# Ninety unread TensorE products in the long waits of a token-table, attention and feed-forward kernel

## The chip, the cores and the metric

One core of a Trainium2 chip runs one program. The metric is the device time in microseconds from start to end of an execution; shown are three runs and one profiled execution.

## What is computed

`x` holds 8 batches of 512 token ids below 2048. Every id is looked up in a codebook of 2048 rows of 256, sent through a two-layer network, then through one attention layer (16 heads of 64, 4 key/value heads, causal, slopes per head) and one low-rank feed-forward layer, each on a normalised input and with a residual:

```python
h = gelu(codebook[x] @ W1 + b1) @ W2 + b2
n = layernorm(h)
q, k, v = n[..., 128:] @ Wq, n[..., 128:] @ Wk, n[..., :128] @ Wv   # q rotated by an angle per head
att = where(causal, q @ k.T / 8 + slope * rel, -inf)
e = exp(att - max(att)); att = e / (1 + sum(e))
h = h + (att @ v) @ Wo
n = layernorm(h)
h = h + gelu((n @ U1) @ V1 + b1f) @ U2 @ V2 + b2f
```

## The kernel before

The first network depends on the id alone, so it is computed once for each of the 2048 codebook rows. The kernel has two program blocks, one behind the other; all engines leave the first before any starts the second.

**Table stage** (`token_table`). Codebook rows go through in 4 chunks of 512. Per chunk TensorE transposes the rows, makes 8 tiles of the hidden layer (`first_product`, lines 480 to 482) and, two steps behind, adds each into the output rows (`second_product`, lines 495 to 497). Matmul operands are split into a high and a low fp32r part, and three products stand for one. VectorE normalises the finished rows, and they are stored to tables in DRAM, of which `early_rows` and `early_values` serve batch 0 alone. Behind its last product TensorE has nothing to do, while VectorE adds the bias, takes the statistics, normalises, and SyncE stores the last chunk and waits for that store.

**Layer stage** (`layer`). The last chunk's value part is made first: four transposes into bank 2 (line 1164), a split by ScalarE (line 834) and VectorE (line 967) and twelve products (line 1171); ScalarE copies them to `vals`, and SyncE stores them (lines 709 and 711). GpSimd meanwhile issues the gathers of batch 0's rows (line 749, four), then, once the value store has landed, those of its values (four) and those of batch 1 (line 732, four). Then come the `opening` products x, k, q: x transposes the gathered rows (line 1034), k and q are products of three parts each (line 1026), and between x and k, and between q and the first scores, ScalarE copies the high part and VectorE makes the low part.

The main loop runs over slots: 8 batches x 16 heads = 128, and 16 more (`SLOTS` = 144) in which the last batch's projection and feed-forward part are done. In a slot TensorE computes the scores (lines 1130 and 1131), VectorE adds the mask and takes the least value (line 910), ScalarE takes exponentials (line 780), VectorE inverts the sums (lines 917, 919), GpSimd scales (line 744), and TensorE, two slots later, transposes the result (line 1142) and, for two slots at a time, multiplies with the values (line 1158). The feed-forward work of a batch is spread by hand over the slots of the next one, by `first(s)` and `second(s)`: w (output projection), y (transposes of the normalised rows, line 1034), u (first low-rank product, six products, line 1026), f (lines 1104 and 1105) and g (line 1110), d. Each engine works its own queue in order, and semaphores tie them.

For the last batch there are no scores beside it. The projection is done in slots 128 to 131; then VectorE takes statistics (line 876), GpSimd the root, VectorE the normalised rows (line 899), and TensorE goes on with y, u, f and g, d, each behind a copy by ScalarE and a split by VectorE. `ALL` is 128 and `LAG` is 2, so slot ALL + 1 + LAG is 131, and ALL + 8 + LAG is 138.

PSUM has 8 banks of 512 columns. Banks 0 and 1 carry hidden tiles in the table stage and scores in the layer stage; banks 2 to 4 hold the transposed probabilities.

Of the kernel before, what the change touches and what calls it, by code (L numbers as in the profile page):

```python
# [11 lines left out]
P = 128  # L12
ROWS, DIM, HID = 2048, 256, 1024
B, T = 8, 512
# [78 lines left out]
def token_table(nc, part, env):  # L93
# [87 lines left out]
    with nc.Block() as block:  # L181
# [276 lines left out]
        def _(pe):  # L458
# [50 lines left out]
            def make_values(i):  # L509
                pe.wait_ge(tok_low, i + 1)  # L510
                pe.wait_ge(wv_low, 1)
                for t in range(NT):
                    dst = ct_bank(1 - t // 2)[:, t % 2 * DIM:(t % 2 + 1) * DIM]
                    at = slice(t * P, (t + 1) * P)
                    pe.matmul(dst, tok_hi[:, at], wv_hi, start=True, stop=False)
                    pe.matmul(dst, tok_lo[:, at], wv_hi, start=False, stop=False)
                    mm = pe.matmul(dst, tok_hi[:, at], wv_lo, start=False, stop=True)
                    if t % 2 == 1:
                        mm.then_inc(v_full, 1)
# [3 lines left out]
            for n in range(STEPS + BEHIND):  # L523
# [8 lines left out]
                if KH <= n < STEPS and n % KH == VALUES_AT:  # L532
                    make_values(n // KH - 1)

ALL = B * HEADS
SLOTS = ALL + HEADS
O_RING = 10
FF_RING = 4
LAG = 2
# [4 lines left out]
def queries_and_keys(s):  # L544

    out = []
    if s % 2 == 0 and s // 2 + 1 < ALL // 2:
        out.append(("q", s // 2 + 1, 0))
    if s % 4 == 1 and (s + 3) // 4 < ALL // REP:
        out.append(("k", (s + 3) // 4, 0))  # L550
# [14 lines left out]
def second(s):  # L565
# [3 lines left out]
    if i >= 1:  # L569
        b = i - 1  # L570
        if b < B - 1 and 1 + LAG <= j < 1 + LAG + NT:
            out.append(("w", b, j - 1 - LAG))
        if s == ALL + 1 + LAG:
            out += [("w", b, 0), ("w", b, 1)]
# [19 lines left out]
def two_banks():  # L594
# [3 lines left out]
    for s in range(SLOTS):  # L598
        out += [("s", s, j) for j in range(len(UNITS))] * (s < ALL)
        out += [use for use in second(s) if use[0] == "f" and use[2] % 4 < 2]  # L600
        out += [("W", B - 1, m) for m in range(2)] * (s == ALL - 1)
    return out
# [6 lines left out]
def layer(nc, part, env):  # L609

    g = env
    ident, causal, slope, bank, idx = g["ident"], g["causal"], g["slope"], g["bank"], g["idx"]
# [32 lines left out]
    start, rows_in, stored = sem("start"), sem("rows_in"), sem("stored")  # L645
# [59 lines left out]
    with nc.Block() as block:  # L705
# [300 lines left out]
        def _(pe):  # L1006
# [43 lines left out]
            def last_ahead(t):  # L1050

                if t % 2 == 0:
                    ring_opened(("W", B - 1, t // 2))
                pe.wait_ge(o_low, PAIRS * B - 2)
                last_products(t, range(PAIRS - 2))

            def product(kind, n, m):
                if kind == "f" and m % 4 < 2:
                    ring_opened((kind, n, m))
                elif kind == "f" and m == 3:  # L1060
                    pe.wait_ge(o_low, min(PAIRS * (n + 1) + 5, PAIRS * B))
                elif kind == "f" and m == 7:
                    pe.wait_ge(ff_made, KF * n + 4)
                elif (kind != "g" or m == 0) and (kind != "w" or n < B - 1):
                    opened((kind, n, m))
                if kind == "q":
                    cols = slice(2 * n % HEADS * D, (2 * n % HEADS + 2) * D)
                    b = n // PAIRS
                    pe.wait_ge(x_low, b + 1)
                    three(a_of("q", n, 0), [((g["wq_hi"][:, cols], g["wq_lo"][:, cols]), (pos_hi[:, b % 2, :], pos_lo[:, b % 2, :]))])\  # L1070
                        .then_inc(q_full, 1)
                if kind == "k":
                    b, c = divmod(n, KVH)
                    pe.wait_ge(x_low, b + 1)
                    three(a_bank, [((both(g["wk_hi"], c), both(g["wk_lo"], c)), (pos_hi[:, b % 2, :], pos_lo[:, b % 2, :]))])\
                        .then_inc(k_full, 1)
                if kind == "x":
                    if n == 0:
                        pe.wait_ge(first_rows_in, 16 * NT)
                    else:  # L1080
                        pe.wait_ge(rows_in, 16 * NT * n)
                    turn_rows(a_of("x", n, m), pos[:, n % 3, :, :]).then_inc(x_full, 1)
                if kind == "w" and n == B - 1:
                    pe.wait_ge(o_low, PAIRS * (n + 1))
                    last_products(2 * m, range(PAIRS - 2, PAIRS))
                    last_products(2 * m + 1, range(PAIRS - 2, PAIRS)).then_inc(w_full, 2)
                elif kind == "w":
                    pe.wait_ge(o_low, PAIRS * (n + 1))
                    tok = slice(m * P, (m + 1) * P)
                    three(c_bank[:, 0:DIM],  # L1090
                          [((o_hi[:, (PAIRS * n + e) % O_RING, tok], o_lo[:, (PAIRS * n + e) % O_RING, tok]),
                            (g["wo_hi"][:, e, :], g["wo_lo"][:, e, :])) for e in range(PAIRS)]).then_inc(w_full, 1)
                if kind == "y":
                    pe.wait_ge(xn_done, norm_no["y", n])
                    turn_rows(y_bank[m], xn[:, :, m * P:(m + 1) * P]).then_inc(y_full, 1)
                if kind == "u":
                    pe.wait_ge(y_low, KD * (n + 1))
                    three(c_bank, [((both(g["u1_hi"], k), both(g["u1_lo"], k)), (y_hi[:, k, :], y_lo[:, k, :]))
                                   for k in range(KD)]).then_inc(u_full, 1)
                if kind == "f":  # L1100
                    pe.wait_ge(u_low, n + 1)
                    cols = slice(m * P, (m + 1) * P)
                    dst = f_bank(n, m)
                    pe.matmul(dst, g["v1_hi"][:, cols], rank_both[:, :], start=True, stop=False)  # L1104
                    pe.matmul(dst, g["v1_lo"][:, cols], rank_both[:, :], start=False, stop=True).then_inc(ff_full, 1)
                if kind == "g":
                    e = KF * n + m
                    pe.wait_ge(ff_made, e + 1)
                    half = slice(m % 2 * D, (m % 2 + 1) * D)
                    pe.matmul(c_bank[half, :], g["u2"][:, m, :], ff[:, e % FF_RING, :], start=m < 2, stop=m >= KF - 2,  # L1110
                              skip_group_check=True, tile_position=(0, m % 2 * D)).then_inc(ff_used, 1)
                if kind == "d":
                    pe.wait_ge(z_low, n + 1)
                    for t in (2 * m, 2 * m + 1):
                        tok = slice(t * P, (t + 1) * P)
                        mm = three(d_bank[m][:, (t % 2) * DIM:(t % 2 + 1) * DIM],
                                   [((z_hi[:, tok], z_lo[:, tok]), (g["v2_hi"][:, :], g["v2_lo"][:, :]))])
                    mm.then_inc(d_full, 1)
# [44 lines left out]
            for t in range(NT):  # L1163
                mm = pe.transpose(bank(2)[:, t * P:(t + 1) * P], tokens[t], ident[:, :])
            mm.then_inc(tok_full, 1)
            pe.wait_ge(tok_low, 1)
            for t in range(NT):
                at, dst = slice(t * P, (t + 1) * P), value_bank(t // 2)[:, t % 2 * DIM:(t % 2 + 1) * DIM]
                three_v = ((tok_hi, wv_hi), (tok_lo, wv_hi), (tok_hi, wv_lo))
                for n, (tok, wv) in enumerate(three_v):  # L1170
                    mm = pe.matmul(dst, tok[:, at], wv, start=n == 0, stop=n == 2)
                if t % 2 == 1:
                    mm.then_inc(last_full, 1)
            for use in opening:
                product(*use)
            for s in range(SLOTS):
                if s < ALL:
                    scores(s, 0)
                    scores(s, 1)
                for use in first(s):  # L1180
                    product(*use)
                if s == ALL:
                    last_ahead(0)
                if 2 + LAG <= s < ALL + 1 + LAG and (s - LAG) % 2 == 0:
                    values(s - 2 - LAG)
                if s < ALL:
                    scores(s, 2)
                turn_ahead = burst(s) or ("u", s // HEADS - 1, 0) in second(s)
                if turn_ahead and LAG <= s < ALL + LAG:
                    turn(s - LAG)  # L1190
                for use in second(s):
                    product(*use)
                if not turn_ahead and LAG <= s < ALL + LAG:
                    turn(s - LAG)
                if ALL <= s < ALL + NT - 1:
                    last_ahead(s - ALL + 1)


# [24 lines left out]
```

## Time and profile before

| | us |
|---|---|
| median of 3 runs | 969.41 |
| lowest, highest | 963.27, 970.1 |
| profiled execution, whole | 972.13 |
| profiled execution, span from first to last instruction | 970.3 |
| TensorE matmul busy | 869.9 (90%) |
| ScalarE busy | 723.7 (75%) |
| GpSimd busy | 630.2 (65%) |
| VectorE busy | 620.2 (64%) |
| mean granted TensorE clock | 0.970 |

The span is the time from the first to the last instruction in the profile. The granted clock is a share of TensorE's full 2.4 GHz; 0.50 is 1.2 GHz. Matmuls overlap, so that the duration of one is longer than the distance to the next one's start. "Idle before" an instruction is the time that its engine stood still, and the arrow names what ended it.

### The profile page before, as it was taken

Reading aid. Unit: us, or ns where it says so; the run is one execution under the profiler, and the core shown is the slowest. Engines: PE = TensorE matmul, PEld = TensorE weight load, DVE = VectorE, ACT = ScalarE, POOL = GpSimd, SP = SyncE. Lnnn points to the kernel's source line nnn. Section 1 sums busy time; section 2 is a strip of 40 time slices with the busy share of each in tenths; the row PEclk is TensorE's granted clock in tenths of the full one; section 3 lists DMA queues with packets and bytes.
Section 4 is the critical chain, followed back from the end, with each engine's and each line's share of the span. In section 5 each row is a group of like instructions: output and inputs, shape, how many; then the busy total and the mean of one; then the engine's idle time right before and its main releaser. Section 6 shows DMA issues by size and latency. Waiting matters only on the chain.

```text
span 970.3 us, 16896 instructions
## 1 busy us (share of the span) xinstructions
PE 869.9 (90%) x5552; PEld 676.4 (70%) x5552; DVE 620.2 (64%) x1898; ACT 723.7 (75%) x1611; POOL 630.2 (65%) x600
## 2 busy tenths in 40 slices
PE   6999658999989998999899998999899989998976
PEld 5888646777866686578657875787667766786663
DVE  4566636876685768575947584867566775668421
ACT  5754347998788867986889687968787788877813
POOL 6000068899685868587858876787759785768520
PEclk9999959999999999999999999999999999999997
DMA  9333350001000200020001000010001000000000
GB/s 258 67 109 109 115 189 2 1 2 55 2 1 2 76 1 1 1 78 1 1 1 57 22 1 1 23 56 1 1 23 55 2 1 23 1 2 1 1 22 22
DMA packets 23605, 33.55 MB, mean 35 GB/s; under 512 B 2608, under 2 KB 20176, under 8 KB 23520
## 3 DMA queue, kind: packets, MB, share of 16 engines
q1 hardware_dynamic: 19760, 19.01, 6.2%
q0 software_dynamic: 3760, 13.48, 4.9%
q8 instruction: 45, 0.74, 0.3%
q14 instruction: 40, 0.33, 0.1%
HBM read 17.80 MB, written 14.68 MB: 33 GB/s over the span
## 4 chain that ended last, share of the span: by engine, by line
PE 48%; DVE 15%; ACT 12%; issue 7%; POOL 5%; DMA 0%; DVEq 0%; POOLq 0%; ACTq 0%
PE ps L1026 14%; PE ps L1158 11%; PE ps L1142 6%; ACT probs L780 6%; DVE probs L910 5%; PE ps L1130 5%; PE ps L1110 4%; PE ps L1131 4%; POOL probs L744 3%; ACT turned_sb L787 3%; DVE sums L917 2%; DVE o_lo L962 2%; DVE xn L899 1%; PE ps L1104 1%; DVE q_both L927 1%
## 5 line engine op out<-in xcount | busy, mean ns | idle before, releaser
L744 POOL TENSOR_SCALAR probs<-probs,sums 128x512 f32<-128x512 f32 (+3 forms) x512 | 545.7, 1083 | 173.7 <-DVE sums L919 173.3
L910 DVE CUSTOM_DVE_ANT_0 probs<-ps,causal,slope 128x512 f32<-128x512 f32 (+3 forms) x512 | 260.0, 548 | 135.7 <-PE ps L1131 131.8
L780 ACT ACTIVATE probs<-probs,least 128x512 f32<-128x512 f32 (+3 forms) x512 | 282.1, 553 | 25.9 <-DVE least L910 19.0
L1130 PE MATMUL ps<-k_hi,q_both 128*128 128x512 f32 (+3 forms) x512 | 184.2, 360 | 28.1 <-DVE least L910 26.1
L787 ACT ACTIVATE turned_sb<-ps 128x1280 f32<-128x1280 f32 x128 | 157.2, 1228 | 69.6 <-PE ps L1142 69.5
L1158 PE MATMUL ps<-turned_sb,token_rows 128*64 128x512 f32 (+3 forms) x1024 | 152.0, 438 | 19.5 <-ACT turned_sb L787 19.4
L1142 PE MATMUL ps<-ident,probs 128*128 128x128 f32 x1280 | 163.0, 275 | 0.3
L1131 PE MATMUL ps<-k_lo,q_both 128*128 128x512 f32 (+3 forms) x512 | 153.5, 325 | 0.0
L1158 PEld LDWEIGHTS ps<-turned_sb,token_rows 128*64 128x64 f32 x1024 | 75.0, 136 | 104.6 <-issue 87.6
L1130 PEld LDWEIGHTS ps<-k_hi,q_both 128*128 128x128 f32 x512 | 97.8, 191 | 71.7 <-DVE least L910 45.7
L1142 PEld LDWEIGHTS ps<-ident,probs 128*128 128x128 f32 x1280 | 144.2, 141 | 1.5 <-POOL probs L744 1.3
L1131 PEld LDWEIGHTS ps<-k_lo,q_both 128*128 128x128 f32 x512 | 98.2, 192 | 5.0
L780 ACT ACTIVATION_READ_ACCUMULATOR probs<-probs,least 128x1 f32 x512 | 96.3, 188 | 0.0
L927 DVE TENSOR_TENSOR q_both<-ps,q_both 64x512 fp32r<-64x512 f32 x128 | 88.1, 688 | 9.7 <-ACT q_both L797 6.3
L797 ACT ACTIVATE q_both<-ps 64x512 fp32r<-64x512 f32 x128 | 75.4, 589 | 16.0 <-PE ps L1026 14.1
L259 POOL TENSOR_TENSOR row_guess<-row_var,row_power 128x4 f32<-128x4 f32 x4 | 4.1, 1026 | 94.6 <-DVE row_var L360 94.6
L1026 PE MATMUL ps<-wo_lo,o_hi 128*128 128x256 f32 x224 | 62.7, 280 | 0.0
L1026 PE MATMUL ps<-wo_hi,o_hi 128*128 128x256 f32 x224 | 62.7, 280 | 0.0
L1026 PE MATMUL ps<-wo_hi,o_lo 128*128 128x256 f32 x224 | 62.7, 280 | 0.0
L962 DVE TENSOR_TENSOR o_lo<-ps,o_hi 128x512 fp32r<-128x512 f32 x64 | 44.3, 691 | 21.1 <-ACT o_hi L829 20.3
L917 DVE TENSOR_SCALAR sums<-sums 128x4 f32<-128x4 f32 x128 | 41.9, 327 | 21.6 <-ACT probs L780 21.3
L408 DVE TENSOR_TENSOR hid_lo<-hid,hid_hi 128x512 fp32r<-128x512 f32 x32 | 22.1, 692 | 39.4 <-ACT hid_hi L310 28.1
(194 smaller groups left out, 1450.2 us busy)
## 6 DMA issues: line engine op xcount, KB each, us to landing
out_dram<-token_rows SPq DMA_DIRECT2D x7, 512.0 KB, 2.9
token_table<-made SPq DMA_DIRECT2D x4, 768.0 KB, 4.0
rows<-in_L_tok_codebook_dram SPq DMA_DIRECT2D x4, 512.0 KB, 9.3
w_f<-in_L_tok_W_dram SPq DMA_DIRECT2D x8, 256.0 KB, 5.0
early_rows<-made SPq DMA_DIRECT2D x4, 512.0 KB, 3.0
early_values<-xn SPq DMA_DIRECT2D x4, 512.0 KB, 3.0
token_table<-xn SPq DMA_DIRECT2D x4, 512.0 KB, 4.4
wo_f<-in_L_attn_Wo_dram POOLq DMA_DIRECT2D x1, 1024.0 KB, 11.1
```

The lines of the kernel that those rows point to most:

```text
L744: ins = pool.tensor_scalar(at, at, recip[:, s % P_RING, q:q + 1], None, ALU.mult)
L780: act.activation(at, at, ACT.Exp, bias=least[:, s % P_RING, q:q + 1], scale=-1.0, accum_out=sums[:, s % P_RING, q:q + 1]).then_inc(exped, 1)
L787: act.activation(turned_sb[:, s % 2, :], turn_ps, ACT.Copy).then_inc(moved, 1)
L797: act.activation(q_both[at, s % 4, :], a_of("q", n, 0)[at, :], ACT.Copy).then_inc(q_high, 1)
L910: dve.tensor_tensor_reduce(out=probs[:, s % P_RING, at], in0=bank(unit % 2)[:, UNIT_AT[q]:UNIT_AT[q] + P * (q + 1)], in1=causal[:, at], sc ...
L927: dve.tensor_tensor(q_both[to, s % 4, :], a_of("q", n, 0)[at, :], q_both[at, s % 4, :].bitcast(F32), ALU.subtract).then_inc(q_low, 1)
L962: dve.tensor_tensor(o_lo[:, p % O_RING, :], o_bank, o_hi[:, p % O_RING, :].bitcast(F32), ALU.subtract)\
L1026: mm = pe.matmul(dst, w, x, start=n == 0, stop=n == len(parts) - 1)
L1130: pe.matmul(dst, w, k_hi[:, slot, 0:P * (q + 1)], start=True, stop=False)
L1131: mm = pe.matmul(dst, w, k_lo[:, slot, 0:P * (q + 1)], start=False, stop=True)
L1142: mm = pe.transpose(turn_ps[:, K_AT[k] + P * (q - k):K_AT[k] + P * (q - k + 1)], probs[:, s % P_RING, Q_AT[q] + P * k:Q_AT[q] + P * (k + 1 ...
L1158: mm = pe.matmul(o_bank[rows, P * k:T], v_rows[:, b % 3, k, n // REP * D:(n // REP + 1) * D], turned_sb[:, (s + e) % 2, K_AT[k]:K_AT[k] + ...
```

## The change

Fillers are added: products of weights that are in SBUF, written to a PSUM bank that holds nothing which is still needed, with no signal and no wait. They all have 128 stationary columns and 512 moving ones, of type fp32r. There are 30 at the end of the table stage's TensorE queue, 5 behind the four transposes of the layer stage, 13 behind the value products, 4 behind x and 4 behind q of the opening; and in the slots of the last batch 20 behind the projection, 6 behind y, 4 behind u and 4 behind f and g. Nothing is removed or moved.

```diff
@@ table stage, TensorE, behind the loop over steps
+            for n in range(30):
+                pe.matmul(hid_bank(1), w1_hi[:, 0, 0:P], w1_hi[:, 0, 0:CH], start=True, stop=True)
@@ layer stage, TensorE
+            def filler(dst, count):
+
+                for n in range(count):
+                    pe.matmul(dst, g["v1_hi"][:, 0:P], g["v1_hi"][:, 0:T], start=True, stop=True)
@@
             mm.then_inc(tok_full, 1)
+            filler(bank(1), 5)
             pe.wait_ge(tok_low, 1)
@@
                 if t % 2 == 1:
                     mm.then_inc(last_full, 1)
+            filler(bank(1), 13)
             for use in opening:
                 product(*use)
+                if use[0] != "k":
+                    filler(bank(1), 4)
@@
                 if ALL <= s < ALL + NT - 1:
                     last_ahead(s - ALL + 1)
+                if s == ALL + 1 + LAG:
+                    filler(bank(2), 20)
+                if s == ALL + 8 + LAG:
+                    filler(bank(2), 6)
+                if s == ALL + 9 + LAG:
+                    filler(bank(2), 4)
+                if s == ALL + 10 + LAG:
+                    filler(bank(2), 4)
```

## Rows read from the trace of the kernel before

**Rows 1.** The page's 40 slices: granted TensorE clock in tenths.

```profile
PEclk9999959999999999999999999999999999999997
```

**Rows 2.** Stretches: length, busy (x) of PE, PEld, DVE, ACT, POOL; clock, DMA share, GB/s.

```profile
118.00:141.00 23.00, 11.38 (x36) 8.85 (x37) 8.02 (x24) 6.79 (x12) 10.47 (x12) 0.50 0.51 159
...
145.50:148.70 3.20, 3.18 (x9) 2.69 (x9) 1.73 (x5) 1.20 (x3) 3.20 (x4) 0.53 0.02 8
...
384.00:388.00 4.00, 4.00 (x15) 3.33 (x14) 0.69 (x3) 1.86 (x8) 2.54 (x3) 0.57 0.00 0
...
786.80:790.20 3.40, 1.48 (x12) 1.36 (x13) 3.37 (x10) 1.85 (x6) 3.06 (x3) 1.00 0.01 2
889.00:893.00 4.00, 4.00 (x15) 3.27 (x14) 0.79 (x3) 1.93 (x8) 2.64 (x3) 0.57 0.02 6
944.00:957.00 13.00, 8.11 (x22) 5.88 (x22) 3.74 (x9) 4.79 (x7) 2.35 (x1) 0.50 0.00 0
```

**Rows 3.** Timeline, block change: start, us, engine, line, operation [idle before <-releaser].

```profile
122.69 1.09 PE L1164 MATMUL ps<-ident,scratch 128*128 128x128 f32 x4 [8.78 <-PEq L181]
...
125.48 0.58 PE L1171 MATMUL ps<-y_hi 128*128 128x256 f32 x1 [1.70 <-DVE y_lo L967]
...
129.07 0.36 SPq L709 DMA_DIRECT2D early_values<-xn  x1
```

**Rows 4.** Timeline, TensorE's x transposes of the opening.

```profile
130.83 1.12 PE L1034 MATMUL ps<-ident,token_rows 128*128 128x128 f32 x4 [2.42 <-DMA token_rows<-early_rows,idx]
```

**Rows 5.** The chain that ended last, k and q products: start, us, what.

```profile
133.36 2.94 PE ps L1026 x6
```

**Rows 6.** Timeline, first scores, third dip, GpSimd's scaling.

```profile
137.69 0.80 PE L1130 MATMUL ps<-k_hi,q_both 128*128 128x512 f32 x1 [1.40 <-DVE q_both L927]
...
138.95 0.75 DVE L910 CUSTOM_DVE_ANT_0 probs<-ps,causal,slope 128x512 f32<-128x512 f32 x1 [0.59 <-PE ps L1131]
...
143.31 8.53 POOL L744 TENSOR_SCALAR probs<-probs,sums 128x512 f32<-128x512 f32 x8
...
145.52 0.80 PE L1026 MATMUL ps<-pos_hi,wk_hi 128*128 128x512 f32 x1 [1.75 <-DVE q_both L927]
...
148.06 0.75 DVE L910 CUSTOM_DVE_ANT_0 probs<-ps,causal,slope 128x512 f32<-128x512 f32 x1 [0.77 <-PE ps L1131]
...
155.45 1.56 POOL L744 TENSOR_SCALAR probs<-probs,sums 128x512 f32<-128x512 f32 x1 [3.61 <-DVE sums L919]
```

**Rows 7.** Timeline, a batch in the middle at full clock: y transposes, u products.

```profile
780.90 0.63 PE L1034 MATMUL ps<-ident,xn 128*128 128x128 f32 x4 [0.99 <-DVE xn L899]
...
790.23 0.47 PE L1026 MATMUL ps<-y_hi,u_hi 128*128 128x512 f32 x1
...
790.53 0.39 PE L1026 MATMUL ps<-y_hi,u_lo 128*128 128x512 f32 x1
790.76 0.39 PE L1026 MATMUL ps<-y_lo,u_hi 128*128 128x512 f32 x1
...
791.89 0.60 ACT L813 ACTIVATE rank_both<-ps 128x512 fp32r<-128x512 f32 x1 [0.77 <-PE ps L1026]
```

**Rows 8.** Timeline, TensorE's y transposes of the last batch.

```profile
945.88 1.94 PE L1034 MATMUL ps<-ident,xn 128*128 128x128 f32 x8 [6.33 <-DVE xn L899]
```

**Rows 9.** The chain that ended last, u, f and g of the last batch.

```profile
949.32 2.91 PE ps L1026 x6
...
953.73 0.77 PE ps L1104
...
957.48 1.03 PE ps L1110 x4
```

**Rows 10.** The same chain: VectorE's statistics, once for each batch.

```profile
261.89 1.33 DVE stats L876 x4
...
362.26 1.33 DVE stats L876 x4
...
464.51 1.33 DVE stats L876 x4
```

## The prediction

> **What bounds the kernel now.** I read the page's slices of the span first: the granted clock of TensorE, the busiest engine, stands at nine tenths or more of full speed in all of them but one early and the last [rows 1]. Next comes the table of stretches. From 118 to 141 us the clock is at 0.50, which is the lower of its two levels (1.2 instead of 2.4 GHz), with TensorE busy half of the time; from 944 to 957 us it is at 0.50 again; and there is a short third dip at 145.5 to 148.7 us [rows 2]. What TensorE did before: it ends the table stage at 113.9 us and stands idle 8.78 us until the second program block lets its transposes start at 122.69 us [rows 3]; behind the last output projection it stands idle 6.33 us [rows 8]. So both long falls follow a wait of TensorE, and the work right behind the wait runs at half speed.
>
> Half speed costs only what the chain of work then passes through. In front, all before 130.83 us hangs on a transfer: the x transposes wait for gathered rows [rows 4], whatever TensorE does. From there the chain goes x transposes, ScalarE and VectorE splits, six products for k and q (2.94 us), splits, scores [rows 5, 6]. At the end it is a bare chain on one batch: transposes, u products, f and g products, and nothing else runs beside it [rows 8, 9]. That is where a faster clock counts in full.
>
> **The change, part by part.** It adds 30+5+13+4+4 products in front (4 behind x and 4 behind q) and 20+6+4+4 at the end, 90 in all, each 128x512 with operands of the fp32r type. No product, wait, transfer or other engine's instruction is removed. The direct gain of the added work is nil; its effect is the clock of what follows.
>
> *Price of a filler.* The nearest row is the same form, a 512-column fp32r product at full clock: u products start at 790.53 and 790.76 us, 0.23 us apart [rows 7]. At the low clock six take 2.91 us with the first one's start included, some 0.43 apart [rows 9].
>
> *Do they hide?* Each stands in front of a wait, so it costs nothing while it ends first.
> - 30 x 0.23 = 6.9 us from 113.9 gives 120.8, against 122.69 [rows 3]: 1.9 us to spare. If TensorE came late to the block's end, everything would start later; that needs 8.8 / 30 = 0.29 us apiece.
> - 5 x 0.23 = 1.2 us behind four transposes, which take 0.63 at full clock [rows 7], end at about 124.5; the value products wait for VectorE until 125.48 [rows 3].
> - 13 x 0.23 = 3.0 us. The twelve value products have 256 columns, half a 512-column one, so 12 x 0.21 = 2.6 us at the low clock and 12 x 0.12 = 1.4 at full [rows 7, 9], to about 126.9; fillers end at 129.9, against 130.83 [rows 4].
> - 4 x 0.23 = 0.9 us behind x, where TensorE waits 133.36 - 131.95 = 1.4 us, and behind q, where the row gives 1.40 [rows 4, 5, 6].
> - At the end 20 x 0.23 = 4.6 of 6.33 us [rows 8]; six (1.4) in the wait before u, 949.32 - 947.82 = 1.5 us, which grows to about 1.8 when the transposes shorten; four (0.9) before f, 953.73 - 952.23 = 1.5 us [rows 8, 9]; the last four stand before the d products, behind the same kind of split.
>
> The trace puts fillers 0.23 us apart. The Trainium skill ("TensorE: Matmul & The Clock Gate", Part 1, "Wait — 56ns, not 53.3ns?") has 215.7 ns between 512-column products at full clock. By that the 30 would take 6.5 us and leave 2.3 us idle rather than 1.9; the forecast goes by the row.
>
> *What full clock gives in front.* Four x transposes 1.12 -> 0.63 [rows 4, 7]: 0.49. Six k and q products, 2.94 us; six u products of that form take 790.23 to 791.89, 1.66 us [rows 5, 7]: 1.28. First scores to VectorE's first piece, 137.69 to 138.95, 1.26 us [rows 6]; a pair at full clock is 0.30 to the second start (790.23 to 790.53), 0.39 for that one and 0.02 for the signal [rows 7], 0.71: 0.55. Sum 2.32. Behind that, ScalarE's exponentials and VectorE carry the chain for a while, and hand the gain on. The third dip lies on the chain too: from 145.52 (three k products, then a pair of scores) to 148.06 is 2.54 us [rows 6]; at full clock 0.30 + 3 x 0.23 + 0.39 + 0.02 = 1.40: 1.14 more. It follows a wait of 1.75 us in thin work [rows 6], which moves; I count it as saved. Together 3.46.
>
> *What could eat it.* GpSimd scales the first two slots from 143.31 for 8.53 us, to 151.84, right behind its gather issues, which don't get faster; it then waits 3.61 us for VectorE's sums until 155.45 [rows 6]. So the gain passes as long as it is below 3.6: just. And ScalarE's copy of the values comes 2.6 - 1.4 = 1.2 us earlier, so the store issued at 129.07 [rows 3] moves to about 127.9 and shares the DMA engines with the last row gather. The trace doesn't show that overlap: between no delay and the whole 1.2 us; I take 0.3, as the engines are half busy (0.51) over the stretch [rows 2]. Front: 3.46 - 0.3 = 3.2.
>
> *What it gives at the end.* y transposes: eight take 1.94 us [rows 8]. Bounds 0.49 (the first four only) and 0.97 (half of all); after the shortening two ScalarE copies and a split in a row bind, so I take 0.6. u: 2.94 -> 1.66, 1.28. f: from 953.73 to the first g at 957.48 is 3.75 us; eight products at 0.23 and 0.07 for the first start, 1.92: 1.83 [rows 7, 9]. From there the clock was already full. End: 3.7.
>
> Sum 6.9 us, with bounds 3.46 - 1.2 + 3.6 = 5.9 and 3.46 + 4.1 = 7.6. The profiled execution took 972.13 us (span 970.3 and 1.8 around it); it would take 965.2. It lies 2.7 us above the median of the runs, 969.41; the same gain gives 962.5.
>
> **Middle of the run.** The clock also falls for a moment in the middle of some batches: 384 to 388 us is the first of four such stretches, each at about 0.57, and 889 to 893 us the last [rows 2]; the other three batches have none. The chain passes VectorE's statistics once per batch: 262 to 362 us takes 100.37, 362 to 464 takes 102.25, the one with the fall [rows 10]. So a fall costs about 1.9 us, and how many a run gets is left to how its waits happen to fall. The change doesn't touch these, but it shifts them.
>
> **The rivals.**
> *The clock falls again in a gap that is left* (1.9 us before 122.69, about 1.7 before the y transposes). For: a 1.75 us wait was followed by a fall at 145 us. Against: the gap is preceded and followed by dense work. In front it would cost nothing (what follows to 130.83 is covered); at the end the y and u steps go back, 0.6 + 1.28 = 1.9: gain 5.0, 964.4 us. From 786.8 to 790.2 us TensorE did ten transposes and two score products in 3.4 us and the clock stayed at 1.00 [rows 2], so transposes behind a gap hold it. The Trainium skill ("TensorE: Matmul & The Clock Gate", Part 4, "PE-mode transpose") says that transpose-mode work does not count as busy for the clock. By that the end's gap and its eight transposes would make one idle piece and this rival would be the forecast; the trace disagrees.
>
> *The front gain is covered*: GpSimd or the gathers are later than I think, and 3.2 us vanish: gain 3.7, 965.7 us. For: GpSimd's margin is only 0.1 us; against: its value gathers come earlier too.
>
> *Two falls fewer in the middle*: 6.9 + 3.8 = 10.7, 958.7 us. *Two more*: gain 3.1, 966.3 us.
>
> *Slower: the fillers themselves run at half clock.* If the clock did not hold over the block change and did not rise again, 13 x 0.43 = 5.6 us from 128.2 end at 133.8, 3.0 behind the gathered rows; 4 x 0.43 = 1.7 exceeds the two waits of 1.4 by 0.3 each; six at the end overrun by 1.1, four by 0.2: 4.9 us lost and nothing gained, 974.3 us. It decides once the 13 take over 0.30 us each. Against: in the third dip TensorE was busy for 3.18 of 3.2 us [rows 2], behind which the clock is up, and fillers are that dense.
>
> **How the numbers follow.** Both stretches at full clock, 962.5: 0.50, own range 961.8 to 963.5. Fall in a left gap: 0.12. Front covered: 0.10. Two fewer falls: 0.13; two more: 0.08. Slower fillers: 0.07. The runs shown reach from 963.27 to 970.1, so the median itself is loose: 963.27 - 6.9 = 956.4 at the low end, 970.1 less the gain with two more falls, 967.0, at the high end. I take 956 to 968. About 1% (9.7 us) is what a measurement of this kernel can tell from no change: below 959.7 lie the case of fewer falls and a little of the main one, 0.16; above 979.1 only a worse form of the last rival, 0.03; within, 0.81.
>
> **What would show it.** Right: granted clock 1.00 from 118 to 141 us and behind 944; x transposes still near 130.8 with 0.63 for four; k and q products 1.7 us; u products 1.7 us; the first statistics of a batch near 258.5; output transfer some 7 us earlier. Wrong: a dip at 122 to 126 or 944 to 948; the x transposes later than 131.2 (the gather lost to the store); "DVE sums" gone as GpSimd's releaser in slots 0 to 2 (the margin gone); a filler as the instruction before a transposes' late start.

## Result and the profile after

| | before | after |
|---|---|---|
| median of the runs, us | 969.31 (20) | 966.76 (20) |
| lowest, highest | 963.27, 973.03 | 962.85, 969.83 |
| profiled execution, whole | 972.13 | 965.27 |
| its span | 970.3 | 963.5 |
| its mean granted clock | 0.970 | 0.989 |

The ratio of the times is 0.9969, with a 95% interval of 0.9956 to 0.9983: 0.3% faster, 3.0 us where 6.9 were forecast. Here and below the ratio is worked out from the single runs and is not exactly the quotient of the two medians. The two profiled executions lie 6.9 us apart, and that agreement with the forecast is an accident, as the parts below show.

The stretches of the changed kernel that answer to [rows 2]; the columns are the same. The two long low stretches are gone. Two short ones stand among the first slots, at 142 and at 152 us.

```profile
118.00:141.00 23.00, 14.59 (x71) 11.06 (x71) 8.08 (x24) 10.50 (x24) 13.18 (x14) 1.00 0.61 188
142.00:145.20 3.20, 2.85 (x9) 2.29 (x7) 1.67 (x7) 1.20 (x3) 3.20 (x4) 0.50 0.13 53
152.20:155.50 3.30, 3.30 (x14) 3.20 (x15) 1.55 (x8) 2.60 (x10) 3.30 (x4) 0.50 0.00 0
941.00:954.00 13.00, 10.49 (x45) 6.45 (x46) 3.46 (x8) 6.66 (x10) 2.39 (x1) 1.00 0.00 0
```

The front of the changed kernel in the timeline (start, us, engine, line; it answers to [rows 3, 4, 6]). L1063 is the filler, L1172 the first transposes of the layer stage, L1037 the x transposes.

```profile
119.89 0.63 PE L1172 MATMUL ps<-ident,scratch 128*128 128x128 f32 x4 [1.96 <-PEq L181]
...
125.04 0.36 SPq L712 DMA_DIRECT2D early_values<-xn  x1
...
129.24 0.66 PE L1037 MATMUL ps<-ident,token_rows 128*128 128x128 f32 x4 [1.89 <-DMA token_rows<-early_rows,idx]
...
134.40 0.50 PE L1138 MATMUL ps<-k_hi,q_both 128*128 128x512 f32 x1 [0.50 <-DVE q_both L930]
...
135.18 0.75 DVE L913 CUSTOM_DVE_ANT_0 probs<-ps,causal,slope 128x512 f32<-128x512 f32 x1
...
141.63 0.55 PE L1029 MATMUL ps<-pos_hi,wk_hi 128*128 128x512 f32 x1 [1.75 <-DVE q_both L930]
...
143.93 0.75 DVE L913 CUSTOM_DVE_ANT_0 probs<-ps,causal,slope 128x512 f32<-128x512 f32 x1 [0.63 <-PE ps L1139]
...
152.74 2.34 PE L1150 MATMUL ps<-ident,probs 128*128 128x128 f32 x10
```

The x transposes stand 9.35 us behind the block's first transposes, where they stood 8.14 behind them before. From there to VectorE's first piece it is 5.94 us instead of 8.12. The k products of slot 1 run at the low clock again, and ten transposes at 152.74 us take 2.34 us.

The end in the chain that ended last; it answers to [rows 8, 9].

```profile
937.16 1.41 DVE stats L879 x4
...
942.65 0.64 PE ps L1037 x4
...
945.38 1.65 PE ps L1029 x6
...
948.53 0.47 PE ps L1112
...
950.64 1.03 PE ps L1118 x4
```

Here everything came as forecast: six u products in 1.65 us, and f to the first g in 2.11.

Now the two executions cut at four marks, the starts of single instructions: the first transposes of the layer stage, VectorE's first statistics of a batch, and its statistics of the last batch.

| stretch, us | before | after | gain |
|---|---|---|---|
| start to the layer stage's first transposes | 122.69 | 119.89 | 2.80 |
| to the first statistics | 139.12 | 139.17 | -0.05 |
| to the last batch's statistics | 678.57 | 678.09 | 0.48 |
| to the end of the span | 29.9 | 26.3 | 3.6 |

In this pair of profiles the end gave 3.6 us, the front nothing. The 2.80 us at the very start have nothing to do with the change: both kernels are the same there. In the execution before, TensorE waited 1.5 us longer for ScalarE's first hidden tile, and then the clock was low from 15.4 to 18.8 us (0.83 over the stretch from 10 to 20 us); in the one after it was at 1.00. Of the profiles below, those with a fall of the clock around 15 us reach the layer stage at 122.5 us, and all others between 119.6 and 120.6.

```profile
10.00:20.00 10.00, 9.10 (x48) 7.41 (x47) 6.83 (x15) 8.96 (x15) 9.47 (x13) 1.00 1.08 309
```

The same product of the table stage, before and after:

```profile
15.65 0.80 PE L480 MATMUL ps<-ct_hi,w_hi 128*128 128x512 f32 x1 [2.36 <-ACT hid L305]
```

```profile
14.31 0.51 PE L480 MATMUL ps<-ct_hi,w_hi 128*128 128x512 f32 x1 [0.90 <-ACT hid L305]
```

### The profile page after: what moved, and what is told of

It reads as the page before. It is cut to its first block, busy times and chain, and to the rows that moved or that the text cites. A ratio compares the mean times of both kernels' runs of the same rounds, so it can differ in the third digit from the quotient of the medians.

```text
span 963.5 us, 17076 instructions
## 1 busy us (share of the span) xinstructions
PE 882.6 (92%) x5642; PEld 685.8 (71%) x5642; DVE 618.7 (64%) x1898; ACT 723.1 (75%) x1611; POOL 630.3 (65%) x600
## 4 chain that ended last, share of the span: by engine, by line
PE 52%; DVE 15%; ACT 13%; issue 6%; DMA 0%; POOL 0%; DVEq 0%; ACTq 0%; POOLq 0%
PE ps L1029 15%; PE ps L1166 12%; PE ps L1150 7%; ACT probs L783 6%; PE ps L1138 6%; DVE probs L913 5%; PE ps L1139 4%; PE ps L1118 4%; ACT turned_sb L790 3%; DVE sums L920 2%; DVE o_lo L965 2%; DVE xn L902 1%; PE ps L1112 1%; ACT k_hi L805 1%; DVE q_both L930 1%
```

## Experiments

Theory A, formed on these profiles: the whole gain is the end's, and the front's is eaten by a later gather and by falls of the clock in the first slots. Theory B: front and end both give a part. In the tables, "x" is the start of the x transposes and "slots" that of the first statistics, both from the block's first transposes; "middle" runs from there to the last batch's statistics, "end" from those to the end of the span.

### One end alone, and the change once more

```diff
 end_only:   without the 30, 5, 13, 4 and 4 fillers in front
 front_only: without the 20, 6, 4 and 4 fillers of the last batch
```

> Only the 34 fillers of the last batch, none in front. Theory A (the front brings nothing, the whole gain is the end's): 3.6 us below the kernel before, about 965.7 against 969.3, and the stretch from the last batch's statistics to the end takes 26.3 us instead of 29.9. Theory B (the front brings its 2 to 3 us and the end less than its 3.6): under 1.5 us below the kernel before.

> Only the 56 fillers in front, none at the end. Theory A: within 0.7 us of the kernel before; from the first transposes of the layer stage to the first statistics of a batch takes 139 us as before, with the x transposes 1.2 us later against the block's start, and low-clock stretches left among the first slots. Theory B: 2 to 3 us below the kernel before, that stretch about 136.5 us.

> The changed kernel once more, for a second profile and as the partner of the others on the same chip. Theory A: 3 us below the kernel before; from the first transposes of the layer stage to the first statistics 139 us as before, x transposes 9.3 us behind the first transposes, and at least one fall of the clock in slots 1 to 4. If the falls in the first profile were chance, this one has them elsewhere or not at all and the stretch is up to 2.5 us shorter.

| kernel | median, us (before) | ratio (95%) | x | slots | middle | end |
|---|---|---|---|---|---|---|
| before | | | 8.14 | 139.12 | 678.6 | 29.9 |
| changed | 966.76 (969.31) | 0.9969 (0.9956 to 0.9983) | 9.34 | 139.17 | 678.1 | 26.3 |
| changed again | 966.14 (969.07) | 0.9982 (0.9963 to 1.0001) | 8.82 | 138.95 | 678.8 | 26.3 |
| end_only | 967.34 (969.07) | 0.9982 (0.9961 to 1.0003) | 8.12 | 140.39 | 678.9 | 26.3 |
| front_only | 969.57 (969.07) | 1.0012 (0.9997 to 1.0028) | 8.58 | 138.76 | 678.5 | 29.5 |

The front alone is worth nothing that the times show: its interval excludes a gain over 0.03%. The end alone measures the same as the whole change, 1.7 us by its medians instead of the 3.6 that I expected. Its interval is wide enough for 3.6 us and for none, but the end of the profile is the same 26.3 us in each kernel with these fillers, against 29.5 to 29.9 without. Theory B, with its 2 to 3 us of the front, falls. The whole change, measured again, is not clear of no change either (up to 1.0001).

The first of the two falls in the first slots is no chance of one profile. The k products of slot 1 or the scores behind them meet a low clock in each of the eight profiles with the front of the kernel before (before, end_only, mid_only) or of the changed kernel (both of its profiles, front_only, and mid and no20, which come below). The fall at 152 us is chance, or nearly: both profiles of the changed kernel and front_only have it, mid and no20 don't, and end_only, which has no filler in front, has it too:

```profile
153.62 2.34 PE L1147 MATMUL ps<-ident,probs 128*128 128x128 f32 x10
```

The stretch to the first statistics takes 139.1, 140.4 and 140.2 us in the three profiles without front fillers and 138.0 to 139.2 in the five with them, 1.1 us less on average; that is all the front may give. The times of front_only don't show even that, and the record doesn't settle which of the two is right.

### Does the earlier store take the row gather's time?

The x transposes come later than before, by 1.2 us in the first pair of profiles, and the store of the last values was issued 5.15 us behind the block's first transposes instead of 6.38. Three edits move the stores.

```diff
 hold_store:  5 of the 13 fillers stand between the two halves of the value products
+                if t == 2:
+                    filler(bank(1), 5)
 late_table:  before the second store
+            sp.wait_ge(first_rows_in, 16 * NT)
 hold_rows:   before the first store
+            sp.wait_ge(first_rows_in, 16 * NT)
```

> The changed kernel with 5 of its 13 fillers moved between the two halves of the value products, so that TensorE's clock stays up but ScalarE's second copy and with it the store of the values go out 1.2 us later, as in the kernel before. Theory A (the earlier store takes the DMA engines from the last row gather): x transposes 8.1 to 8.3 us behind the block's first transposes instead of 9.3, the first scores at 13.4 instead of 14.5. Rival D (the gather is late for another reason, such as TensorE's own reads): x transposes stay at 9.3.

> The changed kernel, but SyncE issues the second store of the last values (into the table that serves batch 1) only when batch 0's rows have landed. Theory A: half of the bytes that meet the gather are gone, x transposes 0.5 to 1.2 us earlier than 9.3; the total up to 1 us below the changed kernel. Rival D: no change of the 9.3.

> The changed kernel, but SyncE issues both stores of the last values only when batch 0's rows have landed, so nothing of theirs can meet the gather; TensorE's fillers stay as they are. Theory A (the first store, issued 5.15 us behind the block's start instead of 6.38, takes 1.2 us from the gather): x transposes at most 8.2 us behind the first transposes instead of 9.3; the values gathers start later, at about 12.2, so GpSimd's scaling starts 2 us later and part of the gain is lost again behind it. Rival D (TensorE's own reads or writes slow the gather): x transposes stay at 9.3.

| kernel | median, us (before) | ratio (95%) | first store | x | slots | end |
|---|---|---|---|---|---|---|
| changed | 966.76 (969.31) | 0.9969 (0.9956 to 0.9983) | 5.15 | 9.34 | 139.17 | 26.3 |
| late_table | 965.83 (970.44) | 0.9956 (0.9935 to 0.9976) | 5.15 | 9.22 | 136.63 | 26.3 |
| front_only | see above | | 5.68 | 8.58 | 138.76 | 29.5 |
| changed again | see above | | 5.88 | 8.82 | 138.95 | 26.3 |
| before | | | 6.38 | 8.14 | 139.12 | 29.9 |
| hold_rows | 963.75 (970.41) | 0.9934 (0.9910 to 0.9958) | 8.32 | 8.29 | 137.70 | 26.3 |
| hold_store | 964.68 (970.44) | 0.9949 (0.9932 to 0.9967) | 8.51 | 9.74 | 138.65 | 26.3 |

The timeline of hold_rows: the store is issued behind the landing, and the values gather, at 132.41 us, waits for it.

```profile
125.34 1.02 POOL L753 DMA_INDIRECT token_rows<-early_rows,idx  x1 [0.30 <-issue]
...
128.68 0.66 PE L1038 MATMUL ps<-ident,token_rows 128*128 128x128 f32 x4 [0.23 <-DMA token_rows<-early_rows,idx]
128.71 0.36 SPq L713 DMA_DIRECT2D early_values<-xn  x1
...
132.41 1.01 POOL L753 DMA_INDIRECT token_rows<-early_values,idx  x1 [6.05 <-DMA early_values<-xn]
```

The DMA engines' share ahead of the landing, changed kernel first, then hold_rows (length, busy by engine, clock, DMA share, GB/s):

```profile
127.00:129.00 2.00, 0.34 (x2) 0.00 (x0) 0.00 (x0) 0.00 (x0) 0.00 (x0) 1.00 1.02 337
```

```profile
126.00:128.70 2.70, 2.47 (x12) 1.71 (x10) 0.00 (x0) 0.12 (x1) 0.35 (x1) 1.00 0.38 122
```

From the issue of the last row gather to the x transposes it is 3.34 us (128.68 - 125.34), near the 3.19 before the change, and 4.40 in the changed kernel. The clock was low in hold_rows from 121.1 to 124.6 us, so by itself it doesn't clear TensorE. slots_hold_mid does, whose times stand further below: it holds both stores too, it runs all the fillers of this front, and its clock is at 1.00 from 119 to 148 us. There it is 3.40 us:

```profile
127.49 1.01 POOL L753 DMA_INDIRECT token_rows<-early_rows,idx  x1 [0.30 <-issue]
...
130.89 0.66 PE L1038 MATMUL ps<-ident,token_rows 128*128 128x128 f32 x4 [0.92 <-DMA token_rows<-early_rows,idx]
```

So TensorE's reads are not the cause: rival D falls, and the stores cost the gather 1.0 to 1.1 us. With the second store alone held it is 0.1 us, less than the 0.5 that I expected at least. No run holds the first store alone, so how the two share the cost is not shown; either one may be enough.

late_table's other 2.4 us up to the first statistics are the two falls: neither stands in its profile. From the k products of slot 1 to VectorE's first piece it takes 1.6 us instead of 2.3 (below), and from there to the first value products 11.4 instead of 13.1. It has one fall of its own, at 146.3 us, behind that piece, which costs nothing that shows. That the held store kept the falls away is not shown. hold_rows has three falls in the middle of the batches, one fewer than the changed kernel, and four runs; part of its good time (0.9934) is that: its middle takes 676.8 us instead of 678.1.

```profile
141.21 0.50 PE L1030 MATMUL ps<-pos_hi,wk_hi 128*128 128x512 f32 x1 [1.75 <-DVE q_both L931]
...
142.75 0.18 DVE L923 RECIPROCAL sums<-sums 128x4 f32<-128x4 f32 x1
142.84 0.72 DVE L914 CUSTOM_DVE_ANT_0 probs<-ps,causal,slope 128x512 f32<-128x512 f32 x1
```

hold_store did not test the store. The clock fell at 121.5 us, 1.4 us behind the wait that the 30 fillers leave ahead of the block, and stayed low until 128.3:

```profile
121.00:128.00 7.00, 6.23 (x22) 5.03 (x21) 0.69 (x1) 1.64 (x5) 4.11 (x4) 0.53 0.47 126
...
124.32 2.33 PE L1063 MATMUL ps<-v_hi 128*128 128x512 f32 x5
...
127.73 2.26 PE L1063 MATMUL ps<-v_hi 128*128 128x512 f32 x8
...
129.82 0.60 PE L1037 MATMUL ps<-ident,token_rows 128*128 128x128 f32 x4
```

The five fillers took 2.1 us, and the x transposes follow on the last filler with no wait at all, 1.5 us behind their place in hold_rows. That is the slower rival in the small. It shows what a filler costs when it is not covered. A fall at 121 us, of half that length, stands in four more profiles (the changed kernel again, front_only, hold_rows, no20). In the three of them without a held store it comes with a later store (5.6 to 5.9 us behind the block's first transposes) and earlier x transposes (8.6 to 8.8 us instead of 9.3): the value products are slower, and that helps.

### The falls in the first slots

```diff
 slots: into bank 5, which nothing uses before slot 4
+ slot 1: filler(4) ahead of scores(1, 2), filler(6) behind it
+ slot 2: filler(5) ahead of q
+ slot 3: filler(3) ahead of scores(3, 1), filler(5) ahead of scores(3, 2)
```

> The changed kernel and 23 more fillers in front of TensorE's waits in slots 1 to 3 (4 and 6 in slot 1, 5 in slot 2, 3 and 5 in slot 3), into bank 5. Theory A (the front gain was lost to falls of the clock in the thin first slots): no low clock between the block's start and slot 5, the stretch from the first transposes to the first statistics 1.1 + 1.4 = 2.5 us shorter than in the changed kernel, the total 2.5 us below it. Rival C (ScalarE and VectorE carry these slots, the clock there is worth nothing): same time as the changed kernel.

964.75 us against 969.07, ratio 0.9955 (0.9938 to 0.9972). Its x transposes stand at 9.33, the first scores at 14.51 and the store at 5.15 us, as in the first profile of the changed kernel; the first statistics at 137.76 instead of 139.17. The stretches that held the two falls:

```profile
142.00:145.20 3.20, 2.86 (x14) 2.37 (x14) 2.46 (x10) 1.20 (x3) 3.20 (x4) 1.00 0.11 45
152.20:155.50 3.30, 3.08 (x23) 2.55 (x23) 2.12 (x11) 3.30 (x10) 3.30 (x5) 1.00 0.00 0
```

So the falls were a real cost, and rival C (ScalarE and VectorE carry these slots) does not hold for all of them. But only 1.4 of the 2.5 us came. From the k products of slot 1 to VectorE's first piece behind them it is 1.6 us here, in late_table and in slots_late_mid, which have no fall there, against 2.3 in the changed kernel: that fall costs 0.7 us. VectorE sets the end of the stretch then, with its sums and reciprocal. In this profile the 0.7 us are lost again, for the k products start 0.6 us later, as VectorE was later with the q split; why, the profile does not show, and in slots_late_mid, with the same fillers, they are on time. The second fall's price came back in full: from that piece to the first value products it is 11.4 us, against 13.1 in the changed kernel and 11.6 before. Behind it 0.3 us are lost.

### The falls in the middle of the batches

Each of the ten profiles of kernels without fillers there has three to five of them. The edit puts 7 fillers ahead of TensorE's wait in the slot of the u products, into the bank that u fills next, behind an added wait for VectorE's split of y, which reads that bank:

```diff
+                if HEADS <= s < ALL and s % HEADS == 9 + LAG:
+                    pe.wait_ge(y_low, KD * (s // HEADS - 1) + 1)
+                    filler(c_bank, 7)
```

> The changed kernel and 7 fillers in each of seven batches, in front of the 1.9 to 2.2 us wait of TensorE ahead of the u products, into the bank that u fills next. Theory A (a fall there costs 1.5 to 1.9 us and four or five come in every run): no low clock between 200 and 900 us, seven intervals of VectorE's statistics at about 100.4 where there were falls, the total 5 to 7 us below the changed kernel. Rival E (the falls move elsewhere in the batch, or fillers run over their wait): the intervals stay at 101.8.

> The kernel before with only the 7 fillers in each of seven batches, ahead of the u products. Theory A (four falls of 1.5 to 1.9 us in every run of the kernel before): 6 us below the kernel before, 963; seven intervals of the statistics sum to 673.5 us instead of 678.6; front and end as before, 139 to 140 and 29.9 us. Rival: falls come back in another place of the batch and the sum stays over 677.

| kernel | median, us (before) | ratio (95%) | slots | middle | end |
|---|---|---|---|---|---|
| mid | 960.41 (970.44) | 0.9906 (0.9883 to 0.9929) | 139.00 | 673.5 | 26.3 |
| mid_only | 965.39 (970.41) | 0.9946 (0.9927 to 0.9966) | 140.17 | 672.9 | 29.9 |

VectorE's statistics in the chain of mid_only, once for each batch; they answer to [rows 10]. Every step is 100.3 to 100.5 us, and the granted clock from 200 to 900 us is 1.00.

```profile
260.45 1.33 DVE stats L876 x4
360.93 1.33 DVE stats L876 x4
461.37 1.33 DVE stats L876 x4
561.82 1.33 DVE stats L876 x4
662.28 1.33 DVE stats L876 x4
762.62 1.33 DVE stats L876 x4
...
200.00:900.00 700.00, 661.86 (x4302) 502.44 (x4300) 479.61 (x1510) 571.50 (x1314) 531.60 (x490) 1.00 0.06 17
```

49 products that nobody reads give 5.7 us of this stretch in the profile (678.6 to 672.9) and 5.2 by the ratio of the times. That is more than the 90 of the change.

### Are the 20 fillers behind the projection needed?

```diff
-                if s == ALL + 1 + LAG:
-                    filler(bank(2), 20)
```

> The changed kernel without the 20 fillers behind the last projection; the 6, 4 and 4 stay. Theory A (the clock must be kept through the 6.3 us wait): the clock falls in it as before, the six fillers at 0.43 us take 2.6 us and overrun u's wait of 1.5 by about 1 us, the clock comes back at some point of the u products; from the statistics to the end 28 to 29.5 us instead of 26.25. Rival F (the dense fillers behind y alone bring the clock back in time): 27 us or less.

967.86 us against 970.41, ratio 0.9976 (0.9961 to 0.9991). The end takes 27.8 us, between the two expectations. TensorE's timeline:

```profile
942.29 1.94 PE L1037 MATMUL ps<-ident,xn 128*128 128x128 f32 x8 [6.33 <-DVE xn L902]
943.88 2.88 PE L1063 MATMUL ps<-v_hi 128*128 128x512 f32 x6
946.59 0.40 PE L1029 MATMUL ps<-y_hi,u_hi 128*128 128x512 f32 x1
...
948.00 1.09 PE L1063 MATMUL ps<-v_hi 128*128 128x512 f32 x4
```

The clock fell in the long wait. The six fillers ran at 0.43 us and put u 4.30 us behind the transposes, instead of 3.44 before the change and 2.73 with the 20. But they also brought the clock back by the first u product. So the 20 are worth 1.5 us and the other 14 give 2.1 by themselves.

### Together

> The fillers of slots 1 to 3, the late second store and the fillers in the middle together. Theory A: the parts add, 2.0 + 1.0 + 6 us below the changed kernel, about 957. If they share a cause, less than that.

> The changed kernel, the fillers of slots 1 to 3, those in the middle of seven batches, and both value stores held until batch 0's rows have landed. Theory A: x transposes at 8.2 to 8.3 us behind the block's first transposes instead of 9.2 to 9.3, no low clock, 136.1 us from there to the first statistics, the total 0.9 us below the kernel with all of this but only the second store held, near 957.5 (0.987 to 0.988 of the kernel before). Rival G (GpSimd becomes the bound: its scaling starts 2.3 us later behind later value gathers, and its wait for VectorE's sums of slot 2, 1.7 us there, is used up): no gain over that kernel, first statistics at 137 us or later.

| kernel | median, us (before) | ratio (95%) | x | slots | middle |
|---|---|---|---|---|---|
| slots_late_mid | 958.47 (970.44) | 0.9889 (0.9868 to 0.9911) | 9.24 | 136.99 | 673.5 |
| slots_hold_mid | 959.00 (970.39) | 0.9884 (0.9868 to 0.9901) | 8.36 | 138.26 | 673.7 |

The parts nearly add. The row of slices of slots_late_mid's profile has the clock up in every slice:

```profile
PEclk9999999999999999999999999999999999999999
```

Holding the first store too gives x its time back (8.36), but not the slots. That profile is of the slowest of its four runs (962.56 us, the others at most 959.08), and the clock fell in it at 148.4 us. GpSimd's wait for VectorE's sums of slot 2, in slots_late_mid and then in slots_hold_mid:

```profile
150.13 8.50 POOL L748 TENSOR_SCALAR probs<-probs,sums 128x512 f32<-128x512 f32 x8 [1.68 <-DVE sums L923]
```

```profile
154.19 8.52 POOL L748 TENSOR_SCALAR probs<-probs,sums 128x512 f32<-128x512 f32 x8 [0.72 <-DVE sums L923]
```

So rival G is near but not shown: the sums still came last, and a fall spoils the comparison. Either version beats both kernels, and the two can't be told apart.

## Why the prediction was wrong

**End, 3.7 forecast, 3.6 measured: right, by its steps.** Statistics to the end went from 29.9 to 26.3. y transposes to u: 3.44 -> 2.73 (0.7, forecast 0.6). u start to f start: 4.41 -> 3.15 (1.26, forecast 1.28). f to g: 3.75 -> 2.11 (1.64; forecast 1.83, as I gave the eight products 1.92). All fillers fitted their waits.

**Front, direct work, 2.32 forecast, 2.18 measured: right.** From the x transposes to VectorE's first piece 8.12 -> 5.94. VectorE's k split now stands right ahead of its q split and ends last, where ScalarE's copy of q did.

**Gather, 0.3 forecast, 1.2 measured: the term that was mis-sized.** The full upper bound came true in the first profile, as the sign named for it did (x transposes later than 131.2 us, that is 8.5 behind the block's first transposes; they came 9.35 behind). Over the five profiles with this front the x transposes stand at 8.6 to 9.7 us, the latest in mid, so it is 0.4 to 1.6 us, 0.9 on average. I took the mean DMA share of the stretch (0.51) as room. What counts is the share when the last gather's rows move, and with the store that is 1.02; hold_rows, with 0.38, and slots_hold_mid show the cause.

**Third dip, "I count it as saved": the step that failed.** It brought 0.24 us (2.54 -> 2.30) instead of 1.14, because the clock fell there again, at 142 us. The wait ahead of it is 1.75 us in both kernels, since VectorE sets it. Full clock makes TensorE's part of such slots smaller, not its waits. I had seen the wait and said only that it "moves". Nor was 1.14 to be had: in the three profiles with full clock there the stretch takes 1.6 us, not 1.40, as VectorE's reciprocal ends last, so the dip was worth 0.9.

**A second fall in the first slots: missing in the sum.** At 152.2 us, with ten transposes at half speed, it took back 1.5 us: from the scores of slot 2 (1.33 us ahead of the kernel before at 143.93) to the first value products (0.18 behind it at 157.03). So 2.18 + 0.24 - 1.2 leaves 1.2 us, and this fall leaves nothing. slots shows it by its absence. That it stands in the one profile and not in the other is luck: end_only has it without front fillers, mid and no20 have these fillers without it. Against the 3.2 us of the forecast the profiles give the front 1.1 on average: the direct work less the gather, and no third dip.

The rival "the clock falls again in a gap that is left" named the gap ahead of the block and the one ahead of the last batch's y transposes, not the slots where the gain had to pass. The first came true in five of eleven profiles, and cost nothing before x in four of them, as it said; the second in none. Its mechanism was right, the place that mattered is not in it, and its chance of 0.12 was too low.

**Middle.** Untouched, as said. But "how many a run gets is left to how its waits happen to fall" overrated chance: ten profiles without fillers there, the kernel before among them, have three to five falls, so the two rivals with two fewer or two more had too much weight. The price per fall held roughly (1.3 to 1.9 us).

**The rest.** One argument against that rival was wrong. The ten transposes at full clock between 786.8 and 790.2 us are one of seven such places, and in four of the others, in the same profile, the clock fell during the ten transposes, behind the same wait (1.93 to 1.97 us). The first of the four and the one I cited:

```profile
382.94 0.39 PE L1130 MATMUL ps<-k_hi,q_both 128*128 128x256 f32 x1 [1.95 <-DVE least L910]
...
383.28 1.59 PE L1142 MATMUL ps<-ident,probs 128*128 128x128 f32 x10
...
788.72 0.39 PE L1130 MATMUL ps<-k_hi,q_both 128*128 128x256 f32 x1 [1.93 <-DVE least L910]
...
789.07 1.25 PE L1142 MATMUL ps<-ident,probs 128*128 128x128 f32 x10
```

So the trace did not speak against the Trainium skill's rule on transposes ("TensorE: Matmul & The Clock Gate", Part 4, "PE-mode transpose"). The forecast that it would have given for the end did not come true: the clock held through the wait of 1.8 us and the eight transposes behind it in all ten profiles with the 20 fillers. More than that about the rule these runs don't show. The GpSimd rival did not bind in the changed kernel: GpSimd still waited 2.72 us for VectorE's sums of slot 2. The median came out at 966.76 us, inside the range of 956 to 968, which is wide enough to say little; the gain is 3.0 us (1.6 to 4.3 by the interval), not 6.9.

## What to carry to other kernels

Work that nobody reads pays where the chain passes TensorE right behind a long wait with nothing beside it. Here that was the end and the middle of the batches, and hardly the front, though the longest low stretch was there. A clock that is kept up must be followed as far as the chain is thin: behind the last filler come waits that other engines set, and one fall there takes the gain back. And an engine off the chain that becomes faster starts its transfers earlier: look whom they meet.

## What was unexpected of the hardware

- Executions of the same table stage differ by 2.0 to 3.0 us. Three of the fourteen profiles have a fall of the clock around 15 us and reach the layer stage at 122.5 to 122.7 us, the others at 119.6 to 120.6. The fall is half of it: in the kernel before, TensorE starts again at 15.65 us instead of 14.31 (1.3 us later, behind a longer wait for ScalarE), and from there to its next transposes it takes 5.74 instead of 4.32. A pair of profiles that differ in this reads like a gain.
- A wait of TensorE of 1.9 to 2.0 us between dense fillers and the block's first transposes was followed by a fall in five of eleven profiles with the front's fillers, the code up to there being the same; the wait of about 1.8 us ahead of the last batch's transposes never was, in the ten with fillers behind the projection.
- Two stores, the first issued 1.2 us earlier than before, made the last row gather, issued 0.2 us ahead of it, 1.2 us longer (3.19 -> 4.40 us to its first reader). With both held it was 3.34 and 3.40.
